# Value products as 64-row tiles in two PSUM banks, row maxima on the two banks that are left

## The reference, cut to what matters

```
xn = layernorm(x)
s  = attention_A(xn)                 # 16 heads of 8, causal, then layernorm and a projection
g  = silu(block_B(xn))               # rmsnorm, 16 query heads on 4 key heads, causal, gate,
                                     # then 8 experts of which each token takes one
out = x + s * g
```

## Time and profile before

| | |
|---|---|
| time, median of 3 runs | 764.24 us (763.57 to 766.36) |
| the profiled execution: its time, its span | 764.92 us, 763.1 us |
| PE busy | 663.1 us, 87% |
| ACT busy | 573.3 us, 75% |
| DVE busy | 534.2 us, 70% |
| POOL busy | 185.0 us, 24% |
| mean granted PE clock | 0.968 of full |
| instructions | 30748, of them 13319 matmuls |

### The profile page before, as it was taken

How to read it: one execution, slowest core, us unless ns; L and a number is a source line. 1 busy time by engine, 2 the same in 40 slices (tenths; PEclk the granted TensorE clock), 3 DMA queues, 4 the chain that set the end, 5 groups by cost and what they waited for, 6 DMA issues and landing times.

```text
span 763.1 us, 30748 instructions
## 1 busy us (share of the span) xinstructions
PE 663.1 (87%) x13319; PEld 226.8 (30%) x13319; DVE 534.2 (70%) x1238; ACT 573.3 (75%) x682; POOL 185.0 (24%) x358
## 2 busy tenths in 40 slices
PE   2267888999999999999999999887978899999993
PEld 1122222322222323222332232232323222355542
DVE  6985532788888677777778788666778688445437
ACT  1166869788878898889878888765766688888881
POOL 5272304101031103110311031010212156125340
PEclk9598989999999999999999999999999999999996
DMA  4112224104112000100120002000000051445522
GB/s 132 49 56 64 63 83 156 54 3 92 44 51 64 12 3 21 49 14 2 32 65 10 3 27 64 14 3 3 3 3 2 3 183 46 115 138 153 167 80 77
DMA packets 36578, 41.95 MB, mean 55 GB/s; under 512 B 6508, under 2 KB 26988, under 8 KB 36444
## 3 DMA queue, kind: packets, MB, share of 16 engines
q1 hardware_dynamic: 34772, 36.81, 16.3%
q0 software_dynamic: 1248, 2.57, 1.0%
q10 hardware_dynamic: 424, 0.62, 0.2%
HBM read 29.41 MB, written 10.24 MB: 52 GB/s over the span
## 4 chain that ended last, share of the span: by engine, by line
PE 57%; DVE 16%; ACT 15%; issue 11%; DMA 0%; POOL 0%; POOLq 0%; ACTq 0%; DVEq 0%
PE PS L1063 23%; ACT PR L934 14%; PE PS L1041 13%; PE PS L1005 9%; PE PS L960 7%; DVE MP L1379 5%; PE PS L1073 1%; PE PS L1010 1%; DVE WORKK L1291 1%; DVE WORKK L1253 0%; DMA FRC<-in_front 0%; DVE WORKQ L1271 0%; PE PS L1163 0%; DVE HS L1283 0%; DVE XN L1236 0%
## 5 line engine op out<-in xcount | busy, mean ns | idle before, releaser
L934 ACT ACTIVATE PR<-PS 128x1024 f32<-128x1024 f32 (+1 forms) x576 | 525.6, 977 | 85.7 <-PE PS L1041 81.7
L1379 DVE TENSOR_REDUCE MP<-PS 128x1 f32<-128x512 f32 (+3 forms) x640 | 358.3, 605 | 106.6 <-PE PS L1005 59.3
L1063 PE MATMUL PS<-PR,VA 128*18 128x512 f32 (+3 forms) x2560 | 292.2, 538 | 2.7 <-POOL PR L744 1.4
L1041 PE MATMUL PS<-QA,KA 58*32 58x512 bf16 (+3 forms) x5120 | 238.7, 354 | 27.2 <-ACT PR L934 19.3
L744 POOL TENSOR_SCALAR_AFFINE_SELECT PR<-PR 128x256 f32<-128x256 f32 x256 | 101.9, 420 | 415.5 <-ACT PR L934 410.3
L1005 PE MATMUL PS<-KA,QA 56*32 56x512 f16 (+3 forms) x2560 | 197.8, 349 | 4.6 <-DVE MP L1379 2.9
L1041 PEld LDWEIGHTS PS<-QA,KA 58*32 58x32 f16 x5120 | 70.7, 90 | 170.9 <-ACT PR L934 144.4
L1005 PEld LDWEIGHTS PS<-KA,QA 56*32 56x32 bf16 x2560 | 56.8, 89 | 120.9 <-DVE MP L1379 94.9
L1063 PEld LDWEIGHTS PS<-PR,VA 128*18 128x18 f32 x2560 | 46.6, 96 | 105.6 <-issue 96.6
L1010 PE MATMUL PS<-MASK 64*32 64x128 bf16 x1024 | 53.4, 217 | 0.0
L813 POOL DMA_INDIRECT expert_outputs<-FC,YI x23 | 22.6, 983 | 45.9 <-DVE FC L1537 45.4
(11 more groups left out here) (180 smaller groups left out, 378.4 us busy)
## 6 DMA issues: line engine op xcount, KB each, us to landing
WORKQ<-in_W SPq DMA_DIRECT2D x16, 450.0 KB, 3.4
QA<-q_parts SPq DMA_DIRECT2D x124, 48.0 KB
WORKK<-in_W SPq DMA_DIRECT2D x7, 450.0 KB, 3.6
KA<-k_parts SPq DMA_DIRECT2D x64, 48.0 KB
q_parts<-WORKQ SPq DMA_DIRECT2D x4, 384.0 KB, 2.7
q_parts<-WORKK SPq DMA_DIRECT2D x4, 384.0 KB, 3.4
expert_tokens<-ZERO SPq DMA_DIRECT2D x1, 1483.5 KB, 10.3
KA<-k_shared SPq DMA_DIRECT2D x60, 24.0 KB
```

Of the source, the lines that this page charges most:

```text
L934: act.activation(PR[:, (2 * n + p) % RING, :, 0:w], PS[:, 2 * p:2 * p + 2, 0:w], ACT.Exp)\
L1041: last = pe.matmul(PS[r:r + STRIP, 2 * p + e, start:start + CH - q0], KA[rows, b, kb // BPC, 0 if ffn else p, key:key + STRIP], QA[rows, b ...
L1063: last = pe.matmul(PS[STRIP * hh:STRIP * hh + 2 * VW, 6, q0:CH], VA[:, slot % 2, kb, hh, VW * (1 - place):VW * (3 - place)], PR[:, (2 * n ...
L1379: dve.reduce_max(top, PS[:, BANK["unit", u], 0:w], AX).then_inc(s_mr, 1)
```

## The change

- **Value products.** Each 128-row product becomes two 64-row products on the two halves of the array. The lower half writes bank 6 and the upper half bank 7. `copy_out` copies bank 6 to OT and then adds bank 7 to it, two DVE instructions with a wait between them.
- **Two banks for the rest.** Units take the longer unused of banks 4 and 5, and so do turns and works, which had bank 7 to themselves; "up" stays in bank 4 and "y" moves to 5. Three of the four last projections run after the loop, into banks 0, 1 and 2; before, two of them did.
- **Maxima.** The ten lower blocks of a diagonal chunk are gathered as three units for each head instead of four: "diagonal" (four masked blocks, 512 columns), "second" (512) and "odd" (256). A reduction gives the maxima of two or four blocks at once. These units go in pairs, both halves of the array at once (`max_pair`): PE waits until both banks are free, and signals at the end of the pair. A head group has 144 units instead of 160, 576 in all, and the spreading uses another weight (GAP = 144 in place of 64) and keeps a pair in one part of a step.

The core of the diff (declarations, initialisation and replaced bank numbers are left out):

```diff
-ITEMS = [(qb, kc) for qb in range(T) for kc in range(qb // BPC + 1)]
+ITEMS = []
+for c in range(NC):
+    ITEMS += [(c, i, kc) for i in range(BPC) for kc in range(c)]
+    ITEMS += [(c, "diagonal", c), (c, "second", c), (c, "odd", c)]
+PIECES_OF = {"diagonal": ((0, 0, 1), (1, 1, 1), (2, 2, 1), (3, 3, 1)), "second": ((2, 0, 2), (3, 0, 2)),
+             "odd": ((1, 0, 1), (3, 2, 1))}
+FIRST_ITEM = [min(i for i in range(len(ITEMS)) if ITEMS[i][0] == c) for c in range(NC)]
+LAST_ITEM = [max(i for i in range(len(ITEMS)) if ITEMS[i][0] == c) for c in range(NC)]
+MSLOT = {"diagonal": NC - 1, "second": NC, "odd": NC + 1}
+MSLOTS = NC + 2
...
-    return (qb % BPC + 1) * P if kc == qb // BPC else CH
+    return sum(n for q, k, n in PIECES_OF.get(ITEMS[i][1], ((0, 0, BPC),))) * P
+def paired(i):
+    return ITEMS[i][1] in PIECES_OF
+GAP = 144
...
-        work = HG * sum(item_width(i) + 64 for i in range(len(ITEMS)))
+        work = HG * sum(item_width(i) + GAP for i in range(len(ITEMS)))
...
-                out[n].append((a, u // HG, u % HG))
-                done += item_width(u // HG) + 64
-                u += 1
+                for _ in range(2 if paired(u // HG) else 1):
+                    out[n].append((a, u // HG, u % HG))
+                    done += item_width(u // HG) + GAP
+                    u += 1
...
-    y = x + (len(u) + 1) // 3
+    def cut(x):
+        return x + 1 if 0 < x < len(u) and paired(u[x][1]) and u[x][2] % 2 else x
+    x = cut((len(u) + 2) // 3)
+    y = cut(max(x, (len(u) + 2) // 3 + (len(u) + 1) // 3))
     return u[:x], u[x:y], u[y:]
...
-PROJECT_AT = {at(NG - 1, NS - 2): 0, at(NG - 1, NS - 1): 1}
+PROJECT_AT = {at(NG - 1, NS - 2): 0}
+TAIL = at(NG - 1, NS - 2)
...
-        return min((4, 5, 7), key=lambda bank: max(i for i, use in enumerate(out) if use[1] == bank))
-    ring = [4, 5, 7, 0, 1, 2, 3]
+        return min((5,) if n >= TAIL else (4, 5), key=lambda bank: max(i for i, use in enumerate(out) if use[1] == bank))
+    ring = [4, 5, 0, 1, 2, 3]
...
-            out.append((("turn", ended(n - LAG - 1)), 7, "D"))
+            out.append((("turn", ended(n - LAG - 1)), oldest(), "D"))
...
-                    out.append((("y", k - 2), 7, "D"))
+                    out.append((("y", k - 2), 5, "D"))
             elif (name, k) in [w for ws in FRONT_AT.values() for w in ws]:
-                out.append(((name, k), (4, 5, 7)[free % 3], "A" if name in ("X", "AV") else "D"))
+                out.append(((name, k), (4, 5)[free % 2], "A" if name in ("X", "AV") else "D"))
                 free += 1
             else:
-                out.append(((name, k), 7, "A" if name in ("O", "G", "H", "E", "L") else "D"))
+                out.append(((name, k), oldest(), "A" if name in ("O", "G", "H", "E", "L") else "D"))
...
                 for r in range(0, P, STRIP):
-                    q = qb % BPC * P + r
-                    last = pe.matmul(bank[r:r + STRIP, 0:w], QA[rows, b, c, pr, q:q + STRIP],
-                                     KA[rows, b, kc, pr, 0:w], start=True, stop=kc < c)
-                if kc == c:
-                    pe.wait_ge(s_cm, 1)
-                    for r in range(0, P, STRIP):
-                        last = pe.matmul(bank[r:r + STRIP, w - P:w], MASK[64 * e:64 * e + 64, M_EYE:M_EYE + STRIP],
-                                         MASK[64 * e:64 * e + 64, r // STRIP * P:(r // STRIP + 1) * P], start=False, stop=True)
+                    q = kind * P + r
+                    last = pe.matmul(bank[r:r + STRIP, :], QA[rows, b, c, pr, q:q + STRIP], KA[rows, b, kc, pr, :],
+                                     start=True, stop=True)
                 last.then_inc(s_mm, 1)
                 half[0] = e
+            def max_pair(a, item, hh):
+                c, kind, _ = ITEMS[item]
+                b, u = SLOT_OF[a] % NBUF, unit_number((a, item, hh))
+                diagonal = kind == "diagonal"
+                order = (1 - half[0], half[0])
+                for e in range(2):
+                    free(("unit", u + e))
+                if diagonal:
+                    pe.wait_ge(s_cm, 1)
+                    for e in order:
+                        for r in range(0, P, STRIP):
+                            pe.matmul(PS[r:r + STRIP, BANK["unit", u + e], :].rearrange("p (j s) -> p j s", s=P),
+                                      MASK[64 * e:64 * e + 64, M_EYE:M_EYE + STRIP],
+                                      MASK[64 * e:64 * e + 64, r // STRIP * P:(r // STRIP + 1) * P].unsqueeze(1)
+                                      .broadcast_to([64, BPC, P]), start=True, stop=False)
+                col0, last = 0, {}
+                for q0, k0, n in PIECES_OF[kind]:
+                    for e in order:
+                        rows, pr = slice(64 * e, 64 * e + STACK), UNIT_PAIR[hh]
+                        for r in range(0, P, STRIP):
+                            q = q0 * P + r
+                            last[e] = pe.matmul(PS[r:r + STRIP, BANK["unit", u + e], col0:col0 + n * P],
+                                                QA[rows, b, c, pr, q:q + STRIP],
+                                                KA[rows, b, c, pr, k0 * P:(k0 + n) * P],
+                                                start=not diagonal, stop=not diagonal or q0 == BPC - 1)
+                    col0 += n * P
+                for e in order:
+                    last[e].then_inc(s_mm, 1)
+                half[0] = order[1]
...
-                        last = pe.matmul(PS[STRIP * hh:STRIP * hh + 2 * VW, 6, q0:CH],
-                                         VA[:, slot % 2, kb, hh, VW * (1 - place):VW * (3 - place)],
-                                         PR[:, (2 * n + hh % 2) % RING, hh // 2, start:start + CH - q0],
-                                         start=kb == 0 and place == 0, stop=kb == d + 2 and not more)
+                        for e in range(2):
+                            rows = slice(64 * e, 64 * e + 64)
+                            last = pe.matmul(PS[STRIP * hh:STRIP * hh + 2 * VW, 6 + e, q0:CH],
+                                             VA[rows, slot % 2, kb, hh, VW * (1 - place):VW * (3 - place)],
+                                             PR[rows, (2 * n + hh % 2) % RING, hh // 2, start:start + CH - q0],
+                                             start=kb == 0 and place == 0, stop=kb == d + 2 and not more)
...
-                    if c == 0:
-                        read(pe, ("up", NT - 1))
-                    else:
-                        pe.wait_ge(s_mr, UNITS * NA)
-                    project_first(c, 4 + c)
-            for c in (2, 3):
+                    read(pe, max((use for use in USES if use[1] == 4 and use[2] in ("A", "D")), key=USES.index)[0])
+                    project_first(c, 4)
+            for c in range(1, NC):
                 pe.wait_ge(s_ex, 2 * N)
-                project_first(c, c - 2)
+                project_first(c, c - 1)
...
+                if paired(item):
+                    dve.wait_ge(s_mm, u - hh % 2 + 2)
+                    qs = [q for q, _, _ in PIECES_OF[kind]]
+                    step = qs[1] - qs[0]
+                    top = MP[:, row + qs[0]:row + qs[-1] + 1:step, MSLOT[kind]]
+                    dve.tensor_reduce(top, bank.rearrange("p (j s) -> p j s", j=len(qs)), AX, ALU.max).then_inc(s_mr, 1)
+                else:
+                    dve.wait_ge(s_mm, u + 1)
+                    dve.reduce_max(MP[:, row + kind, kc:kc + 1], bank, AX).then_inc(s_mr, 1)
...
-                dve.tensor_copy(OT[:, j % 2, :], PS[:, 6, :]).then_inc(s_oe, 1)
+                dve.tensor_copy(OT[:, j % 2, :], PS[:, 6, :]).then_inc(s_oh2, 1)
+                dve.wait_ge(s_oh2, j + 1)
+                dve.tensor_tensor(OT[:, j % 2, :], PS[:, 7, :], OT[:, j % 2, :], ALU.add).then_inc(s_oe, 1)
...
-                bank = (4, 5, 0, 1)[c]
+                bank = (4, 0, 1, 2)[c]
```

More of the change, by code:

```diff
@@ L185, in maxima_at @@
     u = MAXIMA[n] if n < N else []
-    x = (len(u) + 2) // 3
-    y = x + (len(u) + 1) // 3
+    def cut(x):
+        return x + 1 if 0 < x < len(u) and paired(u[x][1]) and u[x][2] % 2 else x
+    x = cut((len(u) + 2) // 3)
+    y = cut(max(x, (len(u) + 2) // 3 + (len(u) + 1) // 3))
     return u[:x], u[x:y], u[y:]
 def maxima_end(a, c):
-    return max(n for n in range(N) for u in MAXIMA[n] if u[0] == a and ITEMS[u[1]][0] // BPC == c)
+    return max(n for n in range(N) for u in MAXIMA[n] if u[0] == a and ITEMS[u[1]][0] == c)
 FRONT_AT = {0: [("Q", 1), ("K", 1)], 1: [("P", 4), ("P", 5)], 2: [("X", 3)], 5: [("Q", 2), ("K", 2)],
@@ L237, in oldest @@
     def oldest():
[L238 to L240 removed]
+        return min((5,) if n >= TAIL else (4, 5), key=lambda bank: max(i for i, use in enumerate(out) if use[1] == bank))
+    ring = [4, 5, 0, 1, 2, 3]
     for i, w in enumerate(PROLOGUE):
[L242 removed]
+        out.append((w, ring[i % 6], "A" if w[0] == "X" else "D"))
     free = 0
@@ L247, in bank_uses @@
```

(39 more changed lines are left out.)

21 lines of the change are left out of this document (10 added, 11 removed).

## The result

The changed kernel takes 809.55 us (median of 4 runs, 807.22 to 810.07). The kernel before took 764.02 beside it. The ratio is 1.058, 95% interval 1.056 to 1.060, so it is 45 us slower. The forecast was 780 us, the range 742 to 802: the sign was right, the size was not.

The account below looks back on a forecast made before the run. No engine was full: PE, busy 87%, counted most, with ACT close behind and PE waiting on DVE for banks. Terms -37.6 - 4 + 10.1 + 18 + 19 + 8.5 + 1.4 = +15.4 on 764.9 gave about 780 us, range 742 to 802.

Parts of the forecast that it names:

- switches: Value products on 64-row tiles avoid tile-height changes beside 64-row work, about 0.21 us per value group: -37.6 us.
- copy and add: Next group's value products wait for the longer copy, 0.55 us for 17 groups, 0.7 for the last: +10.1 us.
- units' ring of two banks: Second-part units wait for the bank of the preceding third-part unit, 0.22 us in 81 steps: +18 us.
- shared banks and the end: Expert steps' "up" waits behind works in bank 4, +8.5 us; a third projection after the loop, +1.4 us.
- fewer, fuller units: Maxima: no step has more than four units, where 15 steps had five to seven: -4 us.
- pairs: Gathered pairs wait for both banks, and DVE starts only when both halves are done: +19 us.
- Both last rivals: Gaps not from tile-height changes, 818 us, chance 0.05; float32 on 64 rows takes two turns, 970 us, chance 0.03.
- 21 steps: Steps with two pairs, or two units and a pair, with long reductions: 0.8 us each, 16.8 us.
- eight more: Further steps, holding two "odd" pairs: 0.3 us each, 2.4 us.
- the T and front works: Works put in two banks cost nothing; without cover each T adds one reduction, 16 x 0.3, 5 us.
- DVE keeps up: Rival: DVE empties the two banks in time, ring costs nothing and pairs 4 us: 747 us, chance 0.30.
- It cancels: Rival: ring and pairs cost about 22 us, within 0.5% of now, 764 us, chance 0.12.

Follow-up runs that it names:

- no_add: after_old_units without the wait and the addition of bank 7 behind the copy, upper halves left out of the outputs: 768.40 us.
- two_banks: Kernel before, with its 128-row value products, single copy and ungathered units, but with banks 4 and 5 only, bank 7 unused: 809.75 us.
- after_old_units: Changed kernel with the 160 ungathered units a head group and the spreading of the kernel before; 64-row products, added copy and two banks stay: 781.72 us.
- units_two: Kernel before with the units of the maxima in banks 4 and 5 alone, while turns, "y" and other works keep bank 7: 792.66 us.
- single_units: Changed kernel, same schedule, with each gathered unit issued by itself, waiting for its own bank alone and read when it alone is written: 774.64 us.
- late_banks: Changed kernel with works O, G, H, E, L, T(15) and the turns of the expert steps in bank 5 alone: 7.4 us gained.
- best1: Changed kernel with gathered units issued and spread one by one, and the works of the expert steps in bank 5 as in late_banks: 766.23 us.
- gather3: Kernel before (128-row products, single copy, three banks) with only the diagonal blocks gathered, units issued and spread one by one: 753.74 us, ratio 0.984.

## Why the prediction was right in sign and wrong in size

```
term                               forecast   measured   by
switches                            -37.6      -41.3     no_add against two_banks (768.4 - 809.7)
copy and add                        +10.1      +13.3     after_old_units against no_add
units' ring of two banks            +18        +28.2     units_two against before
shared banks and the end             +9.9      +16.9     two_banks against units_two
fewer, fuller units                  -4         -7.1     single_units against after_old_units
pairs                               +19        +34.9     after against single_units
sum                                 +15.4      +45
```

Each row is a difference of medians, good to 2 to 5 us by the intervals of the ratios; where the runs compared have different runs of the kernel before beside them, those differ by 0.2 us, which the row of the shared banks takes into account.

**The sum itself: a step that failed.** The order of the rows matters, since the crossed runs show that terms interact by 15 us; the rows for units and pairs hold for 64-row products. Taken in the other order the account is this. Giving up bank 7 cost 45.0 us where I had 27.9 (18 + 9.9). Gathering in pairs then cost 12.7 where I had 15 (19 - 4), so by itself it was priced well. The new products with their add gave 12.9 us on top of that, where I had 27.5 (37.6 - 10.1) and where they do give 28.0 without the pairs. I had added the terms as if they were independent, the switches' gain in full beside pairs that stop PE. So of the miss of 29.6 us 17.1 are the bank's and 14.6 this, less 2.3 for the gathering.

**Switches: right.** The drain was 0.10 and 0.12 us in the earlier trace rows, the products stayed at 0.85 to 0.87, and my 37.6 us lie 3.7 from the measurement. Here the trace agrees with what the Trainium skill says ("TensorEngine Tiling (Array Packing)", Key Properties: a switch of the tiling mode drains the engine). Both last rivals, that float32 on 64 rows takes two turns and that the gaps are not the switch, are refuted.

**Copy and add: right in kind, perhaps a little small.** 13.3 us is 0.74 for each of 18, the whole of the 0.68 + 0.06 that I had discounted to 0.55 a group, and my upper bound (12.6 + 0.7). That would mean that PE's order hides none of it; but the difference is good to about 5 us only, so my 10.1 isn't refuted.

**Pairs: wrong size beside the new products; this is the first row that failed.** The second pair did start about 2.0 us after the first (1.95 in the timeline), but PE stood for 1.31 us, not "about 1 us", and DVE then waited 0.65 for the second pair in its turn. That "DVE starts only when both halves are done" I had named, and priced only once, ahead of the first pair. By the table of steps, the joint issue costs 0.88 us in each of 25 steps with two pairs (4.01 - 3.13) and 0.28 in each of 36 steps with one (2.39 - 2.11): 22 and 10 us. Of the 25, the 17 with long reductions cost 0.95 each (my 0.8) and the 8 with two "odd" pairs 0.76 (my 0.3); the five steps with a pair and two units, which I had counted at 0.8 too, cost 0.18. The 36 I had priced at nothing, so what failed is above all "21 steps" and "eight more" as the whole of the places that pay. The run that gave back only DVE's late start lost 20.9 us. I also treated the pairs as a cost beside the ring's, where a pair is the whole ring: a third bank takes 14.5 us off the gathered pairs, old products in both. With three banks and old products, pairs cost 9 us against units issued and spread singly; this 9 and the 35 differ in the products and in the spreading too, so they are no pair to compare.

**Two banks: the term came out larger, the price of a place did not; the second row that failed.** I took 0.22 of 0.5 us in 81 places, counted in the schedule of the changed kernel. Measured with the units alone the ring costs 28.2 us, inside my bound of 35, and the mechanism is the one in the timeline. But units_two has the schedule of before, where the planner's lists hold 136 such places: 0.21 us each. So my 0.22 a place stands as far as these runs tell, and the 28.2 is the ring's cost for ungathered units; a part of what the gathering gives back (the row of 7.1) can be that it leaves fewer places. What the ring alone costs in the changed schedule no run shows. I had discounted the place because "the switches have just given it such slack". units_two has no such slack and paid no more a place, and with two banks and old units the switches still gave their 41.3; so this reason was not what kept the price low.

**Shared banks: right in the expert steps, missed elsewhere.** "8.5 us" there, measured 7.4 (late_banks) and 5.3 (best1). But I costed "the T and front works" at nothing, with 5 us for T if its cover was gone, and the turns outside the expert steps and block B's works I left out of the sum without a word. About 10 us remain between units_two and two_banks once the expert steps are taken off. By the stretches above, half lie in the steps of block B's works and half in the other steps from 34 on, where turns and T works stand; the front works did cost nothing. No run took turns and works apart.

**Fewer, fuller units: right, too small.** 7.1 us with two banks in the schedule of twos (good to about 5 us). Issued and spread singly, the gathering gains 10.2 us with two banks (781.72 - 771.51) and 10.8 with three (gather3).

**The rivals.** *DVE keeps up* gave as its condition that ring and pairs together cost less than 22 us; they cost 63, though DVE was busy for 67% only. *It cancels* came true only for best1, with the pairs undone.

## What to carry to other kernels

Price a buffer by taking it away alone: one bank of three was worth 45 us here, more than the 28 us that it was given up for, and 60 us to units that come in pairs. When a producer fills its whole ring before it signals, it and its reader take turns, however idle either looks on average. Don't add up a gain and a loss on the same engine as if each stood alone: the products that gave 28 us without the pairs gave 13 beside them. And a change with several parts can hold one that wins alone: the gathering, without the other part, made this kernel 1.6% faster.

## What was not expected of the hardware

Little. 64-row float32 products ran eight at once and took as long as four of 128 rows (0.85 us to the next scores, against 0.87 in the earlier trace rows). PE's mean duration of a maximum unit's record hardly moved (381 ns for 512 columns, before and after), and so did DVE's reduction of 512 columns (686 ns after, 685 in the earlier trace rows): what the change lost, it lost in waits, not in slower work.
